# All four heads of a graph attention layer by transposed scores, the second norm's ends on GpSimd, and a diffusion setup by powers of Q

## What is computed

```python
h = x @ fc_in_w.T + fc_in_b                       # layer 0: 8 Euler steps
w_eff = (w * clip(d, 0, 1)) @ w.T
for _ in range(8):
    f = sigmoid(alpha) * 0.5 * (adj @ h - h) + h @ w_eff - h + x
    h = h + f / 8
x = layernorm(x + h)
q, k, v = split(x @ W)                            # layer 1: 4 heads of 32
scores = q @ k.T / sqrt(32) + where(adj == 0, -inf, 0)
x = layernorm(x + softmax(scores) @ v)
```

## Time and profile before

| | |
|---|---|
| median of three runs | 682.69 us (681.02 to 683.04) |
| the profiled execution | 683.51 us |
| its span, first to last instruction | 681.7 us |
| granted TensorE clock, mean | 0.989 of full speed |
| PE, DVE, ACT, POOL busy | 646.5, 456.5, 452.1, 72.9 us |

### The profile page before, as it was taken

How to read it: one execution, slowest core, us unless ns; L and a number is a source line. 1 busy time by engine, 2 the same in 40 slices (tenths; PEclk the granted TensorE clock), 3 DMA queues, 4 the chain that set the end, 5 groups by cost and what they waited for, 6 DMA issues and landing times.

```text
span 681.7 us, 11846 instructions
## 1 busy us (share of the span) xinstructions
PE 646.5 (95%) x3441; PEld 474.3 (70%) x3441; DVE 456.5 (67%) x1308; ACT 452.1 (66%) x1023; POOL 72.9 (11%) x86
## 2 busy tenths in 40 slices
PE   4998799999999999999999999999999999999883
PEld 3776676867777776868686777778686868676541
DVE  3442437568594958677685849485866768496986
ACT  3122146867778686868686776868686868678881
POOL 3110000001010100101010102001010101000001
PEclk9999999999999999999999999999999999999897
DMA  4000021312213130403031221303030312112211
GB/s 112 0 1 16 0 63 47 78 33 67 59 43 83 25 101 12 112 0 100 24 82 41 63 60 36 88 19 104 11 103 10 96 27 73 37 49 62 65 29 48
DMA packets 37695, 35.47 MB, mean 52 GB/s; under 512 B 7840, under 2 KB 24864, under 8 KB 37664
## 3 DMA queue, kind: packets, MB, share of 16 engines
q1 hardware_dynamic: 37664, 35.09, 20.0%
HBM read 5.57 MB, written 4.19 MB: 14 GB/s over the span
## 4 chain that ended last, share of the span: by engine, by line
PE 85%; DVE 8%; issue 3%; ACT 1%; DMA 1%; SPq 0%; POOL 0%; DVEq 0%; POOLq 0%
PE psS L711 9%; PE psO L816 8%; PE psL L697 8%; PE psL L698 8%; PE psL L699 8%; PE psE L801 7%; PE psL L689 5%; PE psL L691 5%; PE psL L690 5%; PE psM L771 4%; PE psE L797 4%; PE psL L762 2%; PE psM L776 2%; PE psS L636 2%; PE psE L636 2%
## 5 line engine op out<-in xcount | busy, mean ns | idle before, releaser
L957 DVE CUSTOM_DVE_ANT_0 Sm<-psS,mask 128x512 f32<-128x512 f32 x256 | 173.1, 687 | 109.2 <-PE psS L711 66.4
L545 ACT ACTIVATE E<-Sm,negmax 128x512 f32<-128x512 f32 x128 | 91.5, 715 | 39.7 <-DVE negmax L957 39.5
L711 PE MATMUL psS<-Ks,Qs 96*128 96x512 f32 x256 | 99.7, 447 | 4.5 <-DVE negmax L957 2.4
L545 ACT ACTIVATE Sm<-Sm,negmax 128x512 f32<-128x512 f32 x128 | 92.4, 727 | 6.6 <-DVE negmax L957 6.6
L588 ACT ACTIVATE ET<-ET 128x512 f32<-128x512 f32 x128 | 77.7, 622 | 0.4 <-DVE ET L992 0.3
L992 DVE TENSOR_TENSOR ET<-psE,maskT 128x512 f32<-128x512 f32 x120 | 77.0, 682 | 1.0 <-PE psE L797 1.0
L478 POOL TENSOR_TENSOR rstd<-var,minus_half 128x4 f32<-128x4 f32 x32 | 32.2, 1007 | 364.9 <-DVE var L940 364.9
L801 PE MATMUL psE<-ident,E 128*128 128x128 f32 x480 | 67.8, 275 | 2.3 <-ACT ET L591 1.5
L591 ACT ACTIVATE ET<-psE 128x512 f32<-128x512 f32 x116 | 68.5, 590 | 0.3 <-PE psE L801 0.3
L711 PEld LDWEIGHTS psS<-Ks,Qs 96*128 96x128 f32 x256 | 45.6, 192 | 28.7 <-issue 14.2
L801 PEld LDWEIGHTS psE<-ident,E 128*128 128x128 f32 x480 | 57.3, 142 | 8.5 <-ACT E L545 1.7
(11 more groups left out here) (158 smaller groups left out, 1100.7 us busy)
## 6 DMA issues: line engine op xcount, KB each, us to landing
Qs<-qh SPq DMA_DIRECT2D x128, 64.0 KB, 2.0
Ks<-kh SPq DMA_DIRECT2D x128, 64.0 KB, 2.0
xin<-in_x_dram SPq DMA_DIRECT2D x16, 256.0 KB, 2.9
Qs<-ql SPq DMA_DIRECT2D x64, 64.0 KB, 2.0
Ks<-kl SPq DMA_DIRECT2D x64, 64.0 KB, 2.0
out_dram<-y SPq DMA_DIRECT2D x16, 256.0 KB, 2.3
E<-in_adj_dram SPq DMA_DIRECT2D x4, 256.0 KB, 4.3
Qs<-Mh SPq DMA_DIRECT2D x16, 4.0 KB
```

What stands on the lines that cost most here:

```text
L545: nc.scalar.activation(row if h < TH else E[:, h % 2, i, :], row, ACT.Exp, scale=-1.0, bias=negmax[:, h * NT + i:h * NT + i + 1], accum_ou ...
L711: mm(psS[i % 2][:, :], Qs[0:KS, h, i * P:(i + 1) * P], Ks[0:KS, h, :], start=True, stop=True).then_inc(s_mm, 1)
L957: V_.tensor_tensor_reduce(out=Sm[:, i % 2, :], in0=psS[i % 2][:, :], in1=mask[:, i, :], scale=-SCALE, scalar=3e38, op0=ALU.add, op1=ALU.mi ...
```

## The change

**Heads.** `TH` goes from 2 to 4: heads 2 and 3 now take the second matmul, the added mask and the exponential in place, like heads 0 and 1. The transposes of `E` and their copies go. The maxima are brought over in two groups (`MG = 2`), heads 0 and 1 by way of `psM`, heads 2 and 3 by way of `psO`, each with its own transpose, split and two DMAs. `STK` now waits for the last `TR` of its head for all four.

**Second norm.** The residual addition (`ADD`) and the subtraction of the mean with the scaling by the inverse deviation (in `LN2A`) go from VectorE to GpSimd.

**Setup.** `recurrence` goes. The powers of Q come by doubling (three fp32 matmuls, `q_powers`), their products with `fc_in_w` by three wide and nine two-column fp32 matmuls (`feature_powers`), and the coefficients are summed on VectorE: 28 scaled additions of 128x128 (`source_terms`) between the powers of P, then nine of 128x130 (`coefficient_sums`). They come out in the orientation that the loop wants, so their nine transposes go. The load of `alpha` is issued first, and `fc_in_w` and `fc_in_b` after `adj`.

**Bias.** The bias term is the same for all sequences. It is now computed once, in the setup and in iteration 0, as `biasT` (128x512), and VectorE adds it where `YT` is read out for the last time (`("J", 1)`, before a ScalarE copy). The matmul L684 goes from the three coefficient blocks.

**Order.** All tables are written anew.

```diff
-TH = 2
+TH = 4
+MG = (TH + 1) // 2
...
 SP_EVENTS = [
-    ("STK", 0, 0, 2), ("STK", 1, 0, 2), ("OUT", 0, 0, 4), ("STK", 2, 0, 2), ("STK", 3, 0, 2), ("XIN", 0, 0, 0),
-    ("MT", 0, 0, 2),
+    ("MT", 0, 0, 2), ("STK", 3, 0, 2), ("XIN", 0, 0, 0), ("STK", 0, 0, 1), ("MT", 1, 0, 2), ("STK", 1, 0, 1),
+    ("OUT", 0, 0, 3), ("STK", 2, 0, 1),
...
+            for k in range(STEPS):
+                nc.gpsimd.tensor_scalar(Rf[:, k, 0:D], ident[:, :], DT if k else DT + 1.0, None,
+                                        ALU.mult).then_inc(v_done, 1)
...
+                    elif kind == "ADD":
+                        pool.wait_ge(x1_kept, b + 1)
+                        pool.wait_ge(c_ev, b + 1 + C_FREE)
+                        nc.gpsimd.tensor_tensor(att[:, :, :], att[:, :, :], x1res[:, parity, :, :],
+                                                ALU.add).then_inc(z_done, 1)
                     elif kind == "LN2A":
                         inverse_root(1, b)
+                        pool.wait_ge(root[1], b + 1)
+                        pool.wait_ge(y_out, 16 * b + Y_FREE)
+                        carry_waits(pool, pool_passed)
+                        for t in range(NT):
+                            ins = nc.gpsimd.tensor_scalar(y[:, t, :], att[:, t, :], mv[:, 1, t, 0:1],
+                                                          rstd[:, 1, t:t + 1], ALU.subtract, ALU.mult)
+                        ins.then_inc(y_done, 1)
...
+            def q_powers(n):
+
+                pe.wait_ge(q_ev, n + 1)
+                k = 1 << n
+                mm(psM[:, 0:k * D], Qp[:, k, :], Qp[:, 1:k + 1, :], start=True, stop=True).then_inc(q_mm, 1)
+
+            def feature_powers():
+
...
+                for c in range(RS // 3):
+                    slots = R_BANKS[c][:, 0:3 * SLOT].rearrange("p (k s) -> p k s", s=SLOT)
+                    mm(slots[:, :, 0:D], fc[:, 0:D], Qp[:, 3 * c:3 * c + 3, :], start=True, stop=True)
+                    for k in range(3):
+                        last = mm(slots[:, k, D:SLOT], Qp[:, 3 * c + k, :], fc[:, D:SLOT], start=True, stop=True)
...
+            def bias_rows(q):
+
+                pe.wait_ge(bias_ev, (2, 6, 9)[q])
+                for k in range(NT):
+                    for part in (PTh, PTl):
+                        last = mm(psM[0:3 * QUAD, :], wcols[q][:, k, 0:3 * QUAD], part[:, PW - 1 if q else 0, k, :],
+                                  start=k == 0 and part is PTh, stop=k == NT - 1 and part is PTl)
...
+            def bias_constant():
+
+                pe.wait_ge(bias_ev, 10)
+                mm(psM[:, :], brow[:, :], wrow[:, :], start=True, stop=True).then_inc(bias_mm, 1)
...
-                mm(bank, rb[0:3 * QUAD, block, :], Wst[0:3 * QUAD, :], start=True, stop=False)
...
                     elif kind == "MT":
-                        pe.wait_ge(m_ev, MPB * (b + 1))
-                        pe.wait_ge(s_max, s_unit(b, TH, 0))
...
+                        if n == 0:
+                            pe.wait_ge(m_ev, MPB * (b + 1))
+                        else:
+                            pe.wait_ge(c_ev, b + C_FREE)
+                        heads = min(2, TH - 2 * n)
+                        pe.wait_ge(s_max, s_unit(b, 2 * n + heads, 0))
...
+                    elif kind == "J":
+                        dve.wait_ge(l0_mm, l0_unit(b, (kind, n)) + 1)
+                        bank = L0_BANK[L0_UNITS.index((kind, n))]
+                        V_.tensor_tensor(YT[:, :], psL[bank][:, :], biasT[:, :], ALU.add).then_inc(l0_ev[bank], 1)
```

More of the change, by code:

```diff
@@ L514, in _ @@
                     power_high(i, m)
+                    if i == 1 and m < NT - 1:
+                        for t in range(2 * m, min(2 * m + 2, NT)):
+                            row_sum(t)
             def split_x(parity, loads):
@@ L692, in coefficients, with apply_power @@
                 return last
-            def apply_power(bank, high, low, i, fresh):
+            def apply_power(bank, high, low, i, fresh, between=None):
                 for k in range(NT):
+                    if k == 2 and between:
+                        between()
                     mm(bank[:, :], high[:, k, :], PTh[:, i, k, :], start=fresh and k == 0, stop=False)
@@ L862, in recurrence @@
[L862 to L871 removed]
+            V_.scalar_tensor_tensor(out=Qp[:, 1, :], in0=psM[:, 0:D], scalar=DT, in1=decay_ident[:, :],
+                                    op0=ALU.mult, op1=ALU.add).then_inc(q_ev, 1)
@@ new lines, in _, with source_terms @@
+            TERMS = [(m, k) for m in range(1, STEPS) for k in range(STEPS - m)]
+            def source_terms(first, last):
+                for n in range(first, last):
+                    m, k = TERMS[n]
+                    before = [q for q, term in enumerate(TERMS[:n]) if term[1] == k]
+                    dve.wait_ge(v_done, 1 + STEPS + (before[-1] + 1 if before else 0))
+                    V_.scalar_tensor_tensor(out=Rf[:, k, 0:D], in0=Qp[:, m, :], scalar=DT * math.comb(m + k, k),
+                                            in1=Rf[:, k, 0:D], op0=ALU.mult, op1=ALU.add).then_inc(v_done, 1)
@@ new lines, in coefficient_sums @@
+            def coefficient_sums():
+                dve.wait_ge(r_mm, 1)
+                dve.wait_ge(v_done, 1 + STEPS + len(TERMS))
+                for k in range(RS):
+                    power_of_q = STEPS - k
+                    src = R_BANKS[power_of_q // 3][:, power_of_q % 3 * SLOT:(power_of_q % 3 + 1) * SLOT]
+                    V_.scalar_tensor_tensor(out=Rf[:, k, :], in0=src, scalar=float(BINOMIAL[k]), in1=Rf[:, k, :],
+                                            op0=ALU.mult, op1=ALU.add).then_inc(r_ev, 1)
```

329 lines of the change are left out of this document (179 added, 150 removed), and 124 rows, old and new, of tables (ACT_DRAIN, ACT_EVENTS, DVE_DRAIN, DVE_EVENTS).

## The result

| | before | after |
|---|---|---|
| median of the fresh runs | 682.87 us (681.02 to 684.93, 4 runs) | 675.23 us (674.9 to 675.69, 4 runs) |
| ratio | 1 | 0.9888, 95% interval 0.9859 to 0.9917 |
| a second comparison, beside later runs | 685.42 us (6 runs) | 674.73 us (4 runs), ratio 0.9846 (0.9817 to 0.9874) |
| span of the profiled execution | 681.7 us | 673.5 us |

One further run of the kernel before, of 730.49 us at a lower granted clock, is in a slow state and left out of the second comparison.

The account below looks back on a forecast made before the run. TensorE was taken to bound loop and mid-opening, VectorE the drain. Gains 23.0 (loop), 3.8 and 4.7 (opening), 0.7 (iteration 1), less 1.4 (iteration 0) and 2.3 (drain), took 28.5 off 683.5: 655.0, median 654 us, range 645 to 669.

Parts of the forecast that it names:

- What bounds it: Whole kernel: TensorE bounds the loop, busy 37.00 of 37.10 us an iteration, and mid-opening; VectorE sets the drain's pace.
- The loop's sum: Loop, TensorE: transposes and bias matmuls go, second matmuls and a maxima transpose come; net 2.09 us less an iteration.
- The waits of 0.45: Loop: TensorE's expected waiting per iteration at three tight places, 0.45 us, with 0 and 1.5 as ends.
- The walk through one iteration: Loop: following the new order with prices found three tight places: `X1T`, head 2's first `TR`, head 2's first score.
- Does VectorE follow?: Loop: VectorE would be busy 30.2 of 35.0 us an iteration, 86% where it was 71%, and follow TensorE.
- rival A: Loop: VectorE becomes the bound, TensorE waits 1.4 us an iteration; 668 us, median 667.5; chance 0.20.
- GpSimd's scaling: Second norm: four 128x128 scalings on GpSimd at 0.3 us each, bounded by 0 and 1.28, making nothing late.
- rival C: Loop: the output waits for GpSimd's scaling and holds SP's queue before head 2's stacking; slower, median 695.5 us; chance 0.04.
- The opening: Setup up to layer 0: 3.8 us gained before the powers of P and 4.7 us after, recurrence gone.
- Rival D: Opening: P^3 waits for VectorE's coefficient sums as long as for the recurrence; 8.5 us missing, 663 us; chance 0.07.
- Iterations 0 and 1: First two iterations: iteration 0 loses 1.4 us to the rest of the bias, iteration 1 gains 0.7 us.
- The drain: End of the kernel: VectorE 1.0 us more, last sequence's GpSimd work 1.0, ScalarE 0.3; 2.3 us lost, 0 to 4.

Follow-up runs that it names:

- before_nobias: Kernel before without the bias matmul L684 ahead of each of the 48 coefficient groups, so without layer 0's bias; ratio 0.9866, span 673.4 us.
- scale_late: Changed kernel with the second norm's scaling back on VectorE, as its own table entry some entries behind the statistics; ratio 0.9862 of the kernel before, median 676.12 us.
- scale_vec: Changed kernel with the second norm's scaling back on VectorE in every sequence, right behind the statistics; ratio 1.0622 of the kernel before, span 726.5 us.
- combined_1: Changed kernel with the edits of opening_moves2 and two_heads_drain, and sequence 15's scaling on VectorE; ratio 0.9757 of the kernel before, span 666.9 us.
- nomask_drain: Changed kernel without the mask's addition in the last two sequences, ScalarE's exponential reading the bank itself; ratio 0.9876 of the kernel before, span 673.4 us.
- opening_moves2: Changed kernel with the last product of powers of Q behind P's transposes and GpSimd's memset of ones behind `Pl`; ratio 0.9818 of the kernel before, span 670.6 us.
- opening_moves: Changed kernel with the last product of powers of Q behind P's transposes and GpSimd's memset of ones ahead of `Pl`; ratio 0.9892 of the kernel before, span 672.6 us.
- combined_2: combined_1 with `Pl` computed ahead of GpSimd's memsets and sequence 14's statistics and scaling earlier on VectorE; ratio 0.9740 of the kernel before, median 666.84 us.
- two_heads_drain: Changed kernel with heads 2 and 3 of the last two sequences back on the old transposes and copies; ratio 0.9841 of the kernel before, span 670.5 us.
- after_again: The changed kernel itself, unaltered, measured once more; ratio 0.9846 of the kernel before, span 673.8 us.

## Why the prediction was wrong, point by point

**What bounds it** was right for the loop: TensorE 458.74 of 465.06 us. For the drain I wrote that VectorE sets the pace, and then added up busy time for VectorE and for ScalarE, each by itself. That is the step that failed by most, 8.3 of the 20.2 us missing.

**The loop's sum** failed by its sizes: 2.09 of steps were 1.66. Three removed bias matmuls measured 0.57, not 0.72 (before_nobias), and the block of `PV`, now cut in two, takes 0.99 + 2.71 = 3.70 instead of 3.57 us. The rest, about 0.15 an iteration, no run tells apart. The waits of 0.45 measured 0.36. The walk through one iteration paid off; 13 times 0.33 is the 4.2 us missing.

**Does VectorE follow?** Right (rival A falls): 30.5 of 35.8 us and TensorE idle 0.49 us. It is near, as scale_late shows: 1.11 us more of work cost 0.33 us, and a wait of 1.2 us in the wrong place 3.9 us (scale_vec, together with the held scaling and a lower TensorE clock).

**GpSimd's scaling** was mis-sized most: four of 0.795 us, not 0.3, inside the bounds of 0 to 1.28. I took the value nearest in shape (a 128x128 write with one factor). In the loop it costs nothing, since the output was not late and rival C would have needed 1.75 us. At the end it is on after's chain, 3.13 for 1.11 us, twice. With the last one back on VectorE the last stretch was 1.9 us shorter (combined_1), but with both back and the rest as in after it was 67.8 us, no shorter (scale_late).

The Trainium skill, "GPSIMD Engine Reference", section 4.1, puts one-input work on GpSimd near line rate and two-input work at about half VectorE's speed. For the residual addition this case's rows agree (GpSimd 1.26 to 1.31, VectorE 0.68 us); for the scaling with a mean and a deviation per row the rows differ, 0.795 against VectorE's 0.34 us, and the measurement decides.

**The opening** (3.4 for 8.5 gained) failed in four steps, worth 5.5 us; the smaller terms were off by up to 0.8 us in both directions. The way to the first power: the last product of powers of Q and its copy lay on it, 1.1 us (first power at 14.60 to 15.40 with them, at 13.60 to 13.73 without). Its price: 2.80 at full clock became 5.46, since the clock fell, as it did in four of seven profiles; which of the two prices a run pays was luck as far as the sum could know. Where the clock stayed it took 3.13, as its second third waits 0.3 us for the low part `PTl` of VectorE, which the sum didn't name (weight loads in nomask_drain):

```profile
15.69 0.75 PEld L698 LDWEIGHTS psS<-PTl,Qs 128*128 128x128 f32 x4 [0.28 <-DVE PTl L967]
```

`Pl` was late only once the power started earlier (opening_moves2). The products with `fc_in_w`: 4.25 us for 3.45, 3.84 at full clock, not mended by any run. The cast: 1.34 for 0.17 us, of which TensorE felt 0.91. With the way and the cast mended, `Pl` early and the clock up, the forecast's start of layer 0 came out (44.48). Rival D is not what happened: it had layer 0 start after 50 us, measured was 49.8, and the coefficient sums weren't late (in opening_moves they stand where they stood, and TensorE doesn't wait behind them).

**Iterations 0 and 1** missed 2.6 us. TensorE waits 3.3 us for one normalisation in both after and combined_2, and from 80 to 110 us it is busy 23.94 of 30:

```profile
PE psM L828 <- DVE x L1043: 3.5, 2, 3.3
PE psS L772 <- DMA Ks<-kl: 1.8, 2, 1.0
```

In before the longest such wait was 2.4 us. Behind the wait of 3.3 us the granted clock falls, which it doesn't anywhere in this part of before. Ten microseconds of before, of after, and of combined_2:

```profile
80.00:90.00 10.00, 7.40 (x34) 5.34 (x33) 5.02 (x17) 2.30 (x5) 1.63 (x2) 1.00 0.02 4
```

```profile
80.00:90.00 10.00, 6.01 (x21) 3.89 (x20) 4.97 (x17) 2.28 (x4) 1.04 (x1) 0.83 0.00 1
```

```profile
75.00:85.00 10.00, 6.02 (x18) 3.78 (x17) 4.68 (x16) 2.28 (x4) 1.04 (x1) 0.71 0.00 1
```

It is at 0.50 from about 86.1 to 89.5 in after and from 79.6 to 86.0 in combined_2. From the first matmul of layer 0 to the first `PV` TensorE is busy 82.09 us of 90.81 in after and 83.32 of 92.24 in combined_2, so 1.2 of the 1.4 us given back are busy time, as a longer stay at the lower clock would make it. No experiment went there: what makes the wait longer than in before stays open, and the part of the clock is argued and not shown.

**The drain** (11.6 lost for 3.3) failed by adding up each engine's instructions up to a fixed place, as if the two ran beside each other. I had VectorE 1.0 later, ScalarE 0.3, the end 1.0. (For ScalarE the sum has 4.4 us more work; by its own prices 16 x 0.622 - 8 x 0.590 is 5.2, and its busy time in the last stretch rose by 7.6, from 35.85 to 43.49.) In fact the new way of a block asks VectorE for a maximum and an addition and ScalarE for two exponentials; both are nearly full from 621 to 636 and from 650 to 657, and the steps between them (second product, addition, exponential; maxima, split, DMA) form one chain through both. Taking VectorE's part away shifts the wait to ScalarE and the maxima (nomask_drain). Meanwhile TensorE idles and its clock falls. Of the 8.3 us, two_heads_drain gives back 1.3 (3.3 against the longest of the five), and the scaling and order of combined_2 2.7 more. Its last stretch of 64.0 is still 4.3 us over the 59.7 of the forecast, and these stay open. The table of the drain was written anew with the change and I did not test its order by itself. Nor did I test SP's queue: in after's chain the stacking's issues take 7.0 us and the landings of `Ks` 4.1, while after_again's chain doesn't go through SP there, so the two ways are about equally late.

The rule of the Trainium skill that transposes don't count as work for the clock ("TensorE: Matmul & The Clock Gate", Part 4) finds no support here: with fewer transposes in the drain the clock was lower (0.80 against 0.87 in the stretches above), and with them back for two heads it was 0.86. The amount of work changed with them, so this is no test of the rule by itself.

## What to carry to other kernels

Where a stretch is bound by two engines in turn, price the chain of one block through both, with the copy or DMA between them, and ask what is late next when one is relieved: leaving out 18 us of VectorE's work gained nothing. Price every input of the first instruction of a phase, not the one that was late before. And an instruction on VectorE that must wait for GpSimd belongs some entries behind the one that starts GpSimd, or it costs all that is queued behind it.

## What the runs showed of the hardware

- GpSimd held VectorE up. A VectorE cast of 128x4 took 1.34 to 1.35 us in all eight profiles in which GpSimd's memset of 1.8 us ran beside it and 0.16 us in the four in which it didn't; it ended with the memset (37.69 and 37.66 in after), which took 1.80 us in either case. One scaling of a 128x128 tile took 1217 instead of about 340 ns beside a GpSimd subtraction. The Trainium skill, "SBUF — State Buffer", section "SBUF: two separate sides", describes an exclusive lock on a pair of ports that the two share; these rows agree.
- TensorE's granted clock fell to 0.50 behind 2.5 to 2.85 us of idling in four of seven profiles of the same instructions, and stayed at 1.00 behind 2.84 us in three. A forecast can give such a place two prices, 3.1 and 4.3 to 5.5 us, and no more.
- GpSimd's subtraction and multiplication with two values per row takes 795 ns for 128x128 (792 to 804 over 64 of them).
